# Attention scores: q and k as two fp32r parts on half-height array tiles, in place of three bf16 parts on the full array

## What is computed

```python
def _L1_attn_ref(x, W_qkv, W_out, b_out):
    HEADS = 8; DIM_HEAD = 16
    qkvt = x @ W_qkv
    q, k, v, t = map(to_heads, jnp.split(qkvt, 4, axis=-1))
    dots = jnp.einsum('bhid,bhjd->bhij', q, k) * scale
    attn1 = jax.nn.softmax(dots, axis=-1)
    out1 = jnp.einsum('bhij,bhjd->bhid', attn1, v)
    ...
```

## Time and profile before

| | us |
|---|---|
| median of 3 runs (2505.27 to 2515.43) | 2513.67 |
| profiled execution, own time | 2517.94 |
| its span, first to last instruction | 2516.0 |
| PE matmuls busy | 2175.5 |
| DVE busy | 1883.6 |
| ACT busy | 1453.4 |
| POOL busy | 1116.9 |

### The profile page before, as it was taken

One profiled execution on the slowest core, in us unless ns is written; L12 is line 12 of the kernel. 1 busy time (PEld: TensorE's weight loads), 2 busy tenths in 40 slices (PEclk: granted clock), 3 DMA queues, 4 the chain that ended last, 5 costly groups with the idle time before them and its releaser, 6 DMA issues.

```text
span 2516.0 us, 33117 instructions
## 1 busy us (share of the span) xinstructions
PE 2175.5 (86%) x11552; PEld 897.6 (36%) x11552; DVE 1883.6 (75%) x2555; ACT 1453.4 (58%) x2833; POOL 1116.9 (44%) x1240
## 2 busy tenths in 40 slices
PE   2589999999999999999999999999999447778843
PEld 1223333323333333323233333333232136666633
DVE  7877888888888888888888888888882256666732
ACT  1157767767776767767776767666667213444420
POOL 4303316163544526162535435263142446777764
PEclk9889999999999999999999999999998668998975
DMA  5412222231313132231313132322012058666659
GB/s 182 133 43 77 66 79 91 80 110 30 107 35 102 44 102 74 79 106 31 110 33 104 36 101 68 93 74 64 17 52 76 26 170 286 208 195 201 213 172 341
DMA packets 109926, 264.83 MB, mean 105 GB/s; under 512 B 23048, under 2 KB 40912, under 8 KB 103184
## 3 DMA queue, kind: packets, MB, share of 16 engines
q1 hardware_dynamic: 87600, 217.77, 27.6%
q0 software_dynamic: 17280, 35.95, 4.1%
q10 hardware_dynamic: 4880, 8.99, 0.9%
HBM read 154.63 MB, written 111.56 MB: 106 GB/s over the span
## 4 chain that ended last, share of the span: by engine, by line
PE 57%; POOL 12%; ACT 10%; DMA 8%; DVE 5%; issue 5%; SPq 1%; ACTq 0%; POOLq 0%; DVEq 0%
PE ps L857 17%; PE ps L845 15%; PE ps L825 12%; ACT region L1114 8%; POOL y_dram L732 5%; PE ps L802 2%; DMA big<-w_dram 2%; DMA y_dram<-region 2%; DVE row_max L1359 2%; DMA region<-y_dram 2%; POOL norm_v L625 1%; POOL region L629 1%; POOL region L628 1%; ACT region L1121 1%; PE ps L889 1%
## 5 line engine op out<-in xcount | busy, mean ns | idle before, releaser
L1359 DVE TENSOR_REDUCE row_max<-ps 128x1 f32<-128x1024 f32 x1024 | 1239.7, 1220 | 270.8 <-PE ps L825 239.4
L1114 ACT ACTIVATE region<-ps 128x512 f32<-128x512 f32 x2048 | 1112.7, 596 | 528.9 <-PE ps L845 509.6
L845 PE MATMUL ps<-big 99*128 99x512 bf16 x2048 | 666.1, 387 | 44.4 <-DMA big<-max_parts 12.8
L825 PE MATMUL ps<-big 96*128 96x512 bf16 x2048 | 617.6, 383 | 29.6 <-DMA big<-k_rows 18.7
L857 PE MATMUL ps<-region 128*32 128x512 f32 x4096 | 551.1, 610 | 0.7 <-ACT region L1114 0.7
L845 PEld LDWEIGHTS ps<-big 99*128 99x128 bf16 x2048 | 159.8, 98 | 696.1 <-ACT region L1114 649.9
L732 POOL DMA_INDIRECT y_dram<-region x284 | 272.8, 960 | 126.2 <-issue 81.6
L617 POOL TENSOR_TENSOR norm_v<-norm 128x8 f32<-128x8 f32 x32 | 6.7, 210 | 650.2 <-DVE norm L1350 650.1
L676 POOL DMA_INDIRECT xs_dram<-region,slot x256 | 254.9, 996 | 81.2 <-issue 71.8
L825 PEld LDWEIGHTS ps<-big 96*128 96x128 bf16 x2048 | 199.4, 99 | 245.3 <-DVE row_max L1359 30.2
L978 PE MATMUL ps<-big 128*128 128x512 f32 x284 | 128.3, 452 | 73.1 <-DMA big<-w_dram 72.5
(11 more groups left out here) (195 smaller groups left out, 2189.4 us busy)
## 6 DMA issues: line engine op xcount, KB each, us to landing
big<-w_dram SPq DMA_DIRECT2D x71, 514.0 KB, 4.6
big<-q_rows SPq DMA_DIRECT2D x32, 768.0 KB, 5.7
big<-k_rows SPq DMA_DIRECT2D x32, 768.0 KB, 8.0
region<-xs_dram SPq DMA_DIRECT2D x71, 264.0 KB, 2.8
region<-y_dram SPq DMA_DIRECT2D x16, 1024.0 KB, 10.5
region<-in_x SPq DMA_DIRECT2D x28, 512.0 KB, 9.3
q_rows<-q_parts SPq DMA_DIRECT2D x16, 768.0 KB, 3.8
k_rows<-k_parts SPq DMA_DIRECT2D x16, 768.0 KB, 3.5
```

The costliest lines, as they stand in the source:

```text
L825: mm = pe.matmul(ps[:, M_BANK + 2 * (n % 2) + c, :], q_stack[k % 2][0:SHIFT_ROW, h, t * P:(t + 1) * P], k_stack[k % 2][0:SHIFT_ROW, h, c * ...
L845: pe.matmul(ps[:, E_BANK + i, :], k_stack[k % 2][:, h, t * P:(t + 1) * P], q_stack[k % 2][:, h, c * BANK:(c + 1) * BANK], start=True, stop ...
L1114: act.activation(probs[:, u % 2, 2 * p + i, :], ps[:, E_BANK + i, :], ACT.Exp, scale=DH ** -0.5).then_inc(exp_done, 1)
L1359: dve.tensor_reduce(row_max[:, n:n + 1], ps[:, at:at + 2, :], AX.XY, ALU.max).then_inc(max_done, 1)
```

## The change

q and k are split in two fp32r parts (high: rounded, low: the rest), and three pairs of parts are kept: 48 rows, with two rows for the shift 50. The stack of a head stands either on partitions 0 to 49 or on 64 to 113 (`lane_of`: heads 0, 1 of a group of four on the lower half, heads 2, 3 on the upper half). A matmul on such a stack is built with a tile of 64 rows by 128 columns of the array, at row 0 or row 64. The order of maximum units alternates between halves (`max_unit`), and in each step scores and maximum halves are issued by turns. The bytes of the stacks stay the same (half the rows, twice the width).

```diff
-PAIRS = 6
+PARTS, PAIRS = 2, 3
+LANES = 2
+LANE = P // LANES
+LANE_HEADS = GROUP // LANES
 SHIFT_ROW = PAIRS * DH
-STACK = SHIFT_ROW + 3
+STACK = SHIFT_ROW + PARTS
...
+def max_unit(n):
+
+    g, i = divmod(n, GROUP_ROWS)
+    lane = 1 - i % LANES
+    of_lane, t = divmod(i // LANES, TILES)
+    return g * GROUP + lane * LANE_HEADS + of_lane, t
...
+        def lane_of(h):
+            return h % GROUP // LANE_HEADS
+
+        def lane_rows(stk, h, rows):
+
+            at = lane_of(h) * LANE
+            return stk[at:at + rows, h // GROUP * LANE_HEADS + h % LANE_HEADS, :]
...
             def load_stacks(k, g):
...
+                for lane in range(LANES):
+                    first_head = g * GROUP + lane * LANE_HEADS
+                    for stk, rows in ((q_stack, q_rows), (k_stack, k_rows)):
...
             def split(k, n):
...
-                link(pool.tensor_copy(parts[:, 0, :], full))
-                link(pool.tensor_tensor(full, full, parts[:, 0, :], ALU.subtract))
-                link(pool.tensor_copy(parts[:, 1, :], full))
-                pool.tensor_tensor(parts[:, 2, :], full, parts[:, 1, :], ALU.subtract).then_inc(qk_split, 1)
+                pool.tensor_tensor(parts[:, 1, :], full, parts[:, 0, :].bitcast(F32), ALU.subtract).then_inc(qk_split, 1)
...
-            def full_scores(k, n):
+            def full_scores(unit, c):
+                k, n = divmod(unit, STEPS)
+                h, t = max_unit(n)
...
+                mm = pe.matmul(ps[:, M_BANK + 2 * (n % 2) + c, :],
+                               lane_rows(q_stack[k % 2], h, SHIFT_ROW)[:, t * P:(t + 1) * P],
+                               lane_rows(k_stack[k % 2], h, SHIFT_ROW)[:, c * BANK:(c + 1) * BANK], start=True, stop=True)
...
-            def scores(k, s):
+            def scores(k, s, i):
                 g, c, t, p = s // 32, s // 16 % 2, s // 2 % TILES, s % 2
...
+                h = g * GROUP + LANE_HEADS * p + i
...
                 for s in range(STEPS):
-                    if here and s + 1 < STEPS:
-                        scores(it, s + 1)
-                    if nxt and s + 1 == STEPS:
-                        scores(it + 1, 0)
-                    for unit in max_units(it, s):
-                        full_scores(unit // STEPS, unit % STEPS)
+                    units = list(max_units(it, s))
+                    for c in range(HALVES):
+                        if here and s + 1 < STEPS:
+                            scores(it, s + 1, c)
+                        if nxt and s + 1 == STEPS:
+                            scores(it + 1, 0, c)
+                        if units:
+                            full_scores(units[0], c)
+                    for unit in units[1:]:
+                        for c in range(HALVES):
+                            full_scores(unit, c)
...
-            def projected(kind, k, c, dst):
+            def projected(kind, k, c, dst, parts):
                 act.wait_ge(side_ready, side_at[kind, k, c] + 1)
                 if c == 0 and k:
                     act.wait_ge(qk_split, 2 * k)
+                    act.wait_ge(rows_out, k * ROWS_INC)
+                act.activation(parts[:, 0, c * BANK:(c + 1) * BANK], side, ACT.Copy).then_inc(q_high, 1)
+                q_highs[0] += 1
+                act.wait_ge(q_high, q_highs[0])
                 act.activation(dst[:, c * BANK:(c + 1) * BANK], side, ACT.Copy).then_inc(side_free, 1)
...
             def shift(k, g):
...
-                then(dve.tensor_scalar(max_parts[:, 0, :], turned_max, -1.0, None, ALU.mult))
-                then(dve.scalar_tensor_tensor(max_rest[:, :], turned_max, -1.0, max_parts[:, 0, :], ALU.mult, ALU.subtract))
-                dve.sem_inc(side_free, 1)
-                then(dve.tensor_copy(max_parts[:, 1, :], max_rest[:, :]))
-                dve.tensor_tensor(max_parts[:, 2, :], max_rest[:, :], max_parts[:, 1, :],
-                                  ALU.subtract).then_inc(max_split, 1)
+                then(dve.tensor_scalar(max_parts[:, 0, :], turned_max, -1.0, None, ALU.mult))
+                then(dve.scalar_tensor_tensor(max_parts[:, 1, :], turned_max, -1.0, max_parts[:, 0, :].bitcast(F32),
+                                              ALU.mult, ALU.subtract))
+                dve.sem_inc(max_split, 1)
```

More of the change, by code:

```diff
@@ L435, in build @@
         FROM_SP = 8
-        LATE_INC = 16 * len(late_consts)
+        ones_rows = [k_stack[n][lane * LANE + SHIFT_ROW:lane * LANE + STACK, :, :] for n in range(2) for lane in range(LANES)]
+        LATE_INC = 16 * (len(late_consts) + len(ones_rows))
         CONST_INC = 16 * len(consts)
-        ROWS_INC = PAIRS * 16
-        STACK_INC = 2 * 16
-        SHIFT_INC = 3 * 16
+        ROWS_INC = 2 * PARTS * 16
+        STACK_INC = 2 * LANES * 16
+        SHIFT_INC = PARTS * LANES * 16
         SENT_INC = TILES * 16
@@ L815, in values_and_z @@
                               stop=True).then_inc(side_ready, 1)
-            def full_scores(k, n):
-                h, t = divmod(n, TILES)
-                if n % GROUP_ROWS == 0:
+            def full_scores(unit, c):
+                k, n = divmod(unit, STEPS)
+                h, t = max_unit(n)
+                if n % GROUP_ROWS == 0 and c == 0:
                     pe.wait_ge(stack_in[k % 2][h // GROUP], (k // 2 + 1) * STACK_INC)
-                unit = k * STEPS + n
                 if unit >= 2:
                     pe.wait_ge(max_done, unit - 1)
-                for c in range(HALVES):
-                    mm = pe.matmul(ps[:, M_BANK + 2 * (n % 2) + c, :], q_stack[k % 2][0:SHIFT_ROW, h, t * P:(t + 1) * P],
-                                   k_stack[k % 2][0:SHIFT_ROW, h, c * BANK:(c + 1) * BANK], start=True, stop=True)
-                mm.then_inc(full_ready, 1)
+                mm = pe.matmul(ps[:, M_BANK + 2 * (n % 2) + c, :],
+                               lane_rows(q_stack[k % 2], h, SHIFT_ROW)[:, t * P:(t + 1) * P],
+                               lane_rows(k_stack[k % 2], h, SHIFT_ROW)[:, c * BANK:(c + 1) * BANK], start=True, stop=True)
+                if c == HALVES - 1:
+                    mm.then_inc(full_ready, 1)
             def turn_maxima(k, g):
@@ L1041, in _ @@
                 act.dma_start(tile, src).then_inc(late_in, 16)
+            act.wait_ge(ones_done, 1)
+            for rows in ones_rows:
+                act.dma_start(rows.rearrange("p h (n c) -> p (h n) c", c=P).bitcast(F32),
+                              ones_r[:, :].bitcast(F32).unsqueeze(1).broadcast_to([PARTS, HEADS // LANES * TILES, P])
+                              ).then_inc(late_in, 16)
             def excite():
@@ L1358, in maximum @@
                 at = M_BANK + 2 * (n % 2)
[L1359 removed]
+                h, t = max_unit(n)
+                dve.tensor_reduce(row_max[:, h * TILES + t:h * TILES + t + 1], ps[:, at:at + 2, :], AX.XY,
+                                  ALU.max).then_inc(max_done, 1)
             def shift(k, g):
```

85 lines of the change are left out of this document (40 added, 45 removed).

## The result

The changed kernel takes 4113.83 us (median of 4 runs, 4083.35 to 4149.17) against 2512.71 (2505.27 to 2515.43): 1.634 times as long [1.620, 1.648], a ratio that leaves the slowest of the four (4149.17) out. The profiled execution took 4092.41 us with a span of 4090.5. The forecast was 2700 (2530 to 2850): the sign was right, the size was wrong by 1400 us.

The account below looks back on a forecast made before the run. PE was taken to bound an image's ten wide cycles, the chain through ACT most others. Cycles 185, last cycles 4, copies 2, start -4: 187 on 2517.9 gives 2705, less 4.3 for the median: 2700 us, range 2530 to 2850.

Parts of the forecast that it names:

- the same clock: Experts' fp32r products, read as pace for attention's matmuls: starts 0.234 us apart against 0.22, adding 0.11 a cycle.
- the first rival: Attention cycles: shape changes and loads cost nothing with 64-row tiles; about 2515 us, anything from 2485 to 2590; chance 0.17.
- Wide cycles: Attention cycles with a 512-column product, ten an image, bound by PE: 0.56 us more each, to about 4.25.
- transposes: Attention cycles with four transposes, twelve an image: from 3.32 us to 3.85, 0.5 more each taken.
- dispatch: The attention cycle with the dispatch counts, one an image: PE's sum 3.66 us, 0.3 more.
- empty ones: Attention cycles without side work, nine an image: the chain through ACT still decides, 3.31 us, no loss.
- The exposed load and the change of shape: Around side work in attention cycles: 0.09 us for each load and each shape change, 2 x (0.09 + 0.09).
- the copies on ACT: Copies of q and k, from 0.60 to 1.25 us, four times an image: hidden but for some 2 us in all.
- The 4 us taken off at the start: Image 1: POOL's split some 5 us earlier lets the shift's DMA land sooner; 4 us saved, bounds 0 and 8.
- The second (overlap): Scores and maxima in attention run side by side after all, each pair saving 0.22 us: 2390 us; chance 0.07.
- the reading of the parity: Attention's issue order: a block's four score and maximum matmuls all stand on one half, so nothing is gained from overlap.
- The third (no load beside a matmul on one half): Attention cycles: six more loads of 0.09 us show in a cycle, 235 us on top, 2935; chance 0.08.

Follow-up runs that it names:

- The first experiment: Kernel before with three pairs of bf16 parts instead of six, 48 and 51 rows on lower-half 64-row tiles: 3569.64 and 3669.61 us, 1.42 and 1.46 times before.
- the run on 128-row tiles: Changed kernel with two heads' stacks on adjacent rows, contracted together as 96 and 100 fp32r rows: 2608.78 us, 1.038 times before.

## Why the prediction was wrong

**The step that failed** is one that the sum took for granted: that the changed cycles run at the clock of the old ones. It took the experts' fp32r rows "the same clock", and it took every start in a block at 0.22 or 0.234, the pace of the full clock. No term stood for the clock, no rival named it, and no bound held it. The runs showed a clock of 0.50 in its place, with starts 0.43 apart, and this accounts for the miss: 1394 us by the two timelines above, 4099 against 4092 measured. That the matmuls, though as long and as many as before, fill half the rows that those before filled was in the diff and on the page of the change; it was used only as an argument for the first rival. The first experiment, with bf16 and the old order, shows that few rows on half-height tiles suffice to lose the clock. The run with a score and a maximum on opposite halves gives it back with the same tiles, so it is tiles on one half at a time that lose it. The run with 66 rows shows that the rows count on 128-row tiles too, and the fill to 99 rows shows it from the other side, at 1.00. How the loss divides between empty rows and the 64-row tile on one half stays open. The Trainium skill (TensorE: Matmul & The Clock Gate, Part 1) says that the clock is set by how busy TensorE has been. Read as the profile's busy time, that fails here: 539.00 us of 539.00 were busy at 0.50.

**What the sum got right**, in the 71 us that are recorded at the full clock. Wide cycles 4.29 against 4.25 forecast, transposes 3.86 against 3.85, dispatch 3.59 against 3.66, empty ones, two of the four, 3.32 against 3.31. Starts on one half 0.23 to 0.24 apart against 0.234. The exposed load and the change of shape, 0.36 a side cycle forecast, 0.34 by the run on 128-row tiles. That is mechanism and not luck, but how the right terms add up is of use only once the clock is known. The part of 0.09 for each load and each change is not shown apart. Outside the cycle model, the copies on ACT were forecast as almost hidden (2 us in all). In the changed kernel PE is so slow that they are; beside it, on opposite halves, they show as waits of 0.46 for the projections. The 4 us taken off at the start didn't come: the first score stands at 137.94 us, 5 later than the 132.98 of before. And the lower end of the forecast's own range was worked out wrong: the shape changes alone are 0.18 a side cycle, 64 us, which leads from 2700 to 2636, not to 2585; nothing hung on it, as the time went the other way.

**The rivals.** The first (changes of shape and loads cost nothing) is refuted by the same rows: side cycles are 0.54 to 0.60 longer at the full clock. The second (overlap) fails in both its forms: matmuls on one half start 0.234 apart and don't overlap, and the reading of the parity, on which the forecast laid its weight, holds. What it drew on is true, though: 64-row tiles on different halves start together, in the run with max_unit turned round. Even there the time is 2547.37 us and not the rival's 2390. The third (no load beside a matmul on one half) falls too. Weight loads of the changed kernel, at the full clock:

```profile
1001.42 0.19 PEld L867 LDWEIGHTS ps<-big 50*128 50x128 f32 x1
1001.65 0.19 PEld L846 LDWEIGHTS ps<-big 48*128 48x128 f32 x1
```

They begin with the matmuls at 1001.42 and 1001.65 on the same half and cost them nothing. The range of 2530 to 2850 ended where the 0.36 for shape is doubled, and left no room for a cost that wasn't priced.

**The parts of the change**, on the first chip: the order -37 us (2473 against 2511); the type with its two copies, on full-height stacks, +136 on top of that (2609), of which the sum without its terms for shape had only a part (it put order and type together at 187 - 128 = 59, where 98 were measured, the clock in this run being 0.97 and not 1.00); the halves the rest, some 1500 us by the changed kernel's own time, of which some 120 by the cycles at the full clock (0.34 x 23 x 15.5) and, as an estimate, nearly all else by the clock.

## What to carry to other kernels

Before a change makes matmuls narrower, put a line into the sum for the clock itself: work in the same number of columns on fewer rows can drop TensorE to half its pace while the profile shows it busy throughout (66 rows lost the clock here, 80 did not). Filling the rows with zeros up to 96, on 128-row tiles, was nearly free in time and held the clock here (1.42 times before became 1.015). On 64-row tiles a second matmul on the other half brought the clock back (1.634 became 1.014 and 1.039). And tell the level by the distance between starts, since the clock row of these traces says nothing ahead of its first record; where two half-height tiles should overlap, follow the half of each matmul through the issue order first.

## What was not expected of the hardware

- TensorE stayed at its lower level for hundreds of microseconds with no gap in its work: 539.00 us of 539.00 busy, clock 0.50, with 48 to 50 rows on 64-row tiles.
- Rows of zeros hold the clock as rows of data do: on 128-row tiles 1.00 with 48 rows of data and zeros up to 96, against 0.98 falling to 0.66 with 64 rows of data and two of zeros.
- The level isn't steady: 109 us at 1.00 and 229 at 0.50 by turns in the short bf16 kernel, each fall at the gate's 8-column products, and a ratio of 1.014 on one chip and 1.039 on another for the same kernel on opposite halves.
- Two fp32r matmuls on opposite halves start less than 0.01 us apart and the next pair follows 0.33 behind the first, as the second matmul followed the first on one half (0.34).
- Two 64-row tiles on opposite halves held the clock at 0.97 to 0.98 where the same tiles on one half at a time ran at 0.50.
- Open: what beside the rows lowers the clock between 66 rows on 128-row tiles and 61 on 64-row tiles on one half, what sets off a change of level, and what is left of the dips when both halves are filled (clock 0.96 to 0.97).
